# Cross-attention and routed experts on one core: four neighbouring rows per partition, VectorE gates each tile when it is ready, GpSimd makes the later expert numbers

## The reference

```python
x = x + xattn(layernorm(x), ctx_1024, W_q, W_kv, W_out, ln_gamma, ln_beta)   # 16 heads of 64, 77 context rows
x = x + ffn(layernorm(x), Wg, bg, W1, b1, W3, b3, W2, b2)                    # 8 experts, d_ff 512, top 2

# ffn
probs = softmax(x @ Wg + bg)
top_v, top_i = top_k(probs, 2);  top_v = top_v / (top_v.sum(-1) + 1e-6)
for e in range(8):
    h = silu(x @ W1[e] + b1[e]) * (x @ W3[e] + b3[e])
    out = out + combine[..., e:e+1] * (h @ W2[e] + b2[e])
```

## Time and profile before

| | |
|---|---|
| median of 3 runs | 160.51 us (160.01 to 161.1) |
| the profiled execution | 159.87 us, of which the span from its first to its last instruction is 157.9 us |
| TensorE busy, share of span | 143.5 us, 91% |
| VectorE busy | 103.3 us, 65% |
| ACT busy | 79.0 us, 50% |
| GpSimd busy | 80.9 us, 51% |
| chain that ended last | TensorE 72%, VectorE 10%, ACT 8%, DMA 3%, "issue" 3% |
| granted TensorE clock | 1.00 of full speed (2.4 GHz) over the span |

### The profile page before, as it was taken

One profiled execution on the slowest core, in us unless ns is written; L12 is line 12 of the kernel. 1 busy time (PEld: TensorE's weight loads), 2 busy tenths in 40 slices (PEclk: granted clock), 3 DMA queues, 4 the chain that ended last, 5 costly groups with the idle time before them and its releaser, 6 DMA issues.

```text
span 157.9 us, 4065 instructions
## 1 busy us (share of the span) xinstructions
PE 143.5 (91%) x1209; PEld 134.5 (85%) x1209; DVE 103.3 (65%) x319; ACT 79.0 (50%) x222; POOL 80.9 (51%) x98
## 2 busy tenths in 40 slices
PE   5986996989999999897989999999997999999990
PEld 5875885779998999896868899999996999999990
DVE  0548599989899977897759875365453363484350
ACT  3179357857464694830544243544754544535031
POOL 3550003948553686214781577777777777535000
PEclk9999999999999999999999999999999999999999
DMA  4999995130000003028953089878437996810454
GB/s 128 328 315 290 248 144 92 34 126 11 2 2 4 0 0 110 27 69 268 286 142 109 17 241 367 274 265 222 154 80 226 328 335 209 268 50 21 132 150 133
DMA packets 23821, 24.50 MB, mean 155 GB/s; under 512 B 2525, under 2 KB 16713, under 8 KB 23801
## 3 DMA queue, kind: packets, MB, share of 16 engines
q1 hardware_dynamic: 20608, 20.57, 44.4%
q0 software_dynamic: 1440, 2.82, 6.4%
q10 hardware_dynamic: 1753, 0.87, 2.0%
HBM read 19.91 MB, written 4.33 MB: 154 GB/s over the span
## 4 chain that ended last, share of the span: by engine, by line
PE 72%; DVE 10%; ACT 8%; DMA 3%; issue 3%; SPq 0%; ACTq 0%; DVEq 0%
PE psum L1378 26%; PE psum L1391 14%; PE psum L1439 9%; PE psum L1421 5%; DMA early<-in_L_xattn_W_kv_dram 3%; PE psum L1154 2%; PE psum L1405 2%; PE psum L1156 2%; PE psum L1155 2%; DVE prob L849 2%; DVE negmax L844 2%; ACT g_room L643 2%; PE psum L1365 2%; PE psum L1288 1%; DVE perm L929 1%
## 5 line engine op out<-in xcount | busy, mean ns | idle before, releaser
L1378 PE MATMUL psum<-probT,w 128*128 128x128 f32 x368 | 45.5, 276 | 2.8 <-issue 1.7
L1378 PEld LDWEIGHTS psum<-probT,w 128*128 128x128 f32 x368 | 43.0, 192 | 3.8 <-issue 2.7
L1096 DVE SCALAR_TENSOR_TENSOR probT<-psum,bias_col,prob 128x128 f32<-128x128 f32 x92 | 26.0, 345 | 28.3 <-ACT prob L743 27.6
L743 ACT ACTIVATE prob<-psum,bias_col 128x128 f32<-128x128 f32 x92 | 26.2, 368 | 35.1 <-PE psum L1378 35.1
L573 POOL DMA_INDIRECT g_room<-xf_scratch,idx x22 | 22.1, 1003 | 15.9 <-issue 6.0
L530 POOL TENSOR_TENSOR prob<-prob,rowsum 128x1232 f32<-128x1232 f32 x8 | 18.0, 2250 | 22.5 <-DVE rowsum L840 22.5
L1391 PE MATMUL psum<-w,probT 128*128 x184 | 25.0, 279 | 0.3 <-DVE probT L1096 0.2
L1391 PEld LDWEIGHTS psum<-w,probT 128*128 128x128 f32 x184 | 22.6, 191 | 0.9 <-issue 0.8
L582 POOL DMA_INDIRECT y_scratch<-xnT,out_row x16 | 16.4, 1023 | 9.8 <-DVE xnT L1105 6.4
L1439 PE MATMUL psum<-vo,probT 128*128 128x128 f32 (+1 forms) x160 | 19.3, 276 | 0.0
L1439 PEld LDWEIGHTS psum<-vo,probT 128*128 128x128 f32 (+1 forms) x160 | 18.5, 192 | 0.0
(11 more groups left out here) (186 smaller groups left out, 203.2 us busy)
## 6 DMA issues: line engine op xcount, KB each, us to landing
w<-in_L_ffn_W_dram SPq DMA_DIRECT2D x54, 256.0 KB, 5.2
early<-in_L_xattn_W_kv_dram SPq DMA_DIRECT2D x2, 512.0 KB, 6.2
y_scratch<-zero_rows SPq DMA_DIRECT2D x2, 512.0 KB, 8.4
x_sb<-in_x_dram SPq DMA_DIRECT2D x2, 256.0 KB, 5.0
early<-in_L_xattn_W_q_dram SPq DMA_DIRECT2D x1, 512.0 KB, 6.1
...
xf_scratch<-xf SPq DMA_DIRECT2D x2, 256.0 KB, 2.6
```

The source lines that it names most:

```text
L743: act.activation(silu[:, j % 2, c, :], psum[:, 2 * (j % 2), c * P:(c + 1) * P], ACT.Silu, bias=bias_col[:, 0, bass.ds(expert, 1), c]).then ...
L1096: dve.scalar_tensor_tensor(out=hT[:, j % 2, c, :], in0=psum[:, 2 * (j % 2) + 1, c * P:(c + 1) * P], scalar=bias_col[:, 1, bass.ds(expert[j ...
L1378: ins = pe.matmul(psum[:, 2 * (j % 2) + a, c * P:(c + 1) * P], w13[:, j % WR, a, c * P:(c + 1) * P], xt[:, j % XR, :], start=True, stop=True)
```

## The change

- **Layout.** Token p * 4 + t of a batch element stands on partition p of tile t: four neighbouring rows per partition. The loads of x, the stores to the scratch of xf, the reads of y_back and the stores of the output follow (`rows_of_half`), as do two constants of token numbers (`row_of`, `iota_n`).
- **Gate weights.** They are stored from `gate_w` as they stand, four numbers per partition, in four DMAs that wait for gate_ok. The transpose, the copy `gateT` and its semaphores go.
- **VectorE's order.** gated(0) follows top_two(2); the bases (`other_bases`) come out of other_tiles and follow gated(0); ranks(2) and blocks_of(2) stand before gated(1); other_tiles and one_hots(2) behind it; bias_down(0) and gated(2) stand before other_rows; the output rows come out of other_rows (`other_out_rows`) and stand behind gated(3).
- **Expert numbers of tiles 5 to 22.** `other_experts` moves from VectorE to GpSimd, as eight instructions, ahead of last_powers and gather(5).
- **Register loads.** VectorE reads the numbers of tiles 0 and 1 behind first_tiles, that of tile 2 behind other_bases; TensorE reads each tile's number right behind the up of the tile before.
- **TensorE's and ACT's order.** The slot rows of the other tiles come behind up(3) instead of up(2); from up(4) on, expert_xT(j + 1) follows up(j).

The diff, cut to what the text speaks of:

```diff
-        out_rows = out.rearrange("b (t p) d -> p (b t) d", p=P)
+        out_rows = out.rearrange("b (p t) d -> p b t d", p=P)
+        def rows_of_half(dram, k, half):
+            row = k * (N + P) + half * BANK
+            return dram[row:row + BANK, :].rearrange("(p t) d -> p t d", p=P)
         OWN_AT = [psum[:, RANK_BANK, :], psum[:, 6, :]]
-        GATE_AT = psum[0:K * T, RANK_BANK, 0:P]
         AFTER = 4
...
         def _(sp):
-            x_v = x.rearrange("b (t p) d -> p (b t) d", p=P)
-            sp.dma_start(x_sb[:, 0:TB, :], x_v[:, 0:TB, :]).then_inc(ld["x0"], 16)
+            x_v = x.rearrange("b (p t) d -> p b t d", p=P)
+            sp.dma_start(x_sb[:, 0:TB, :], x_v[:, 0, :, :]).then_inc(ld["x0"], 16)
             sp.dma_start(wkv_sb[:, 0:INNER], w_kv[:, 0:INNER]).then_inc(ld["wk"], 16)
             sp.dma_start(wq_sb, w_q[:, :]).then_inc(ld["wq"], 16)
-            sp.dma_start(x_sb[:, TB:T, :], x_v[:, TB:T, :]).then_inc(ld["x1"], 16)
+            sp.dma_start(x_sb[:, TB:T, :], x_v[:, 1, :, :]).then_inc(ld["x1"], 16)
             sp.dma_start(wkv_sb[:, INNER:2 * INNER], w_kv[:, INNER:2 * INNER]).then_inc(ld["wv"], 16)
...
                 for t in groups[2]:
-                    row = k * (N + P) + t * P
-                    sp.dma_start(xf_dram[row:row + P, :], zero_rows[:, :]).then_inc(zero_st, 16)
+                    sp.dma_start(rows_of_half(xf_dram, k, t // TB)[:, t % TB, :], zero_rows[:, :]).then_inc(zero_st, 16)
...
                 for k in range(K):
-                    row = k * (N + P) + g.start * P
-                    sp.dma_start(xf_dram[row:row + len(g) * P, :].rearrange("(t p) d -> p t d", p=P),
+                    sp.dma_start(rows_of_half(xf_dram, k, g.start // TB)[:, g.start % TB:g.start % TB + len(g), :],
                                  xf[:, g.start:g.stop, :]).then_inc(xf_st[n // 2], 16)
...
                 elif j == 2 * FULL + 4:
-                    sp.wait_ge(gateT_ok, 1)
+                    sp.wait_ge(gate_ok, 1)
                     for k in range(K):
-                        row = k * (N + P)
-                        sp.dma_start(gate_dram[row:row + N, :].rearrange("(t p) o -> t (p o)", p=P),
-                                     gateT[k * T:(k + 1) * T, :]).then_inc(gate_st, 16)
+                        for half in range(B):
+                            sp.dma_start(rows_of_half(gate_dram, k, half).rearrange("p t o -> p (t o)"),
+                                         gate_w[:, k, half * TB:(half + 1) * TB]).then_inc(gate_st, 16)
                 expert_weights(j)
...
             for k in range(K):
-                row = k * (N + P)
-                sp.dma_start(y_back[:, k, 0:TB, :],
-                             y_dram[row:row + BANK, :].rearrange("(t p) d -> p t d", p=P)).then_inc(back[0][k], 16)
+                sp.dma_start(y_back[:, k, 0:TB, :], rows_of_half(y_dram, k, 0)).then_inc(back[0][k], 16)
             sp.wait_ge(o_ok, 1)
-            sp.dma_start(out_rows[:, 0:TB, :], xn[:, 0:TB, :]).then_inc(stored, 16)
+            sp.dma_start(out_rows[:, 0, :, :], xn[:, 0:TB, :]).then_inc(stored, 16)
             sp.wait_ge(stored, 16 * B)
...
                           allow_small_or_imprecise_dtypes=True).then_inc(const_ok, 1)
-                pool.iota(row_of[:, :, :], pattern=[[P, T], [N + P, K]], base=-PAD_ROW, channel_multiplier=1,
+                pool.iota(row_of[:, :, :].rearrange("p (b t) k -> p b t k", b=B), pattern=[[BANK, B], [1, TB], [N + P, K]],
+                          base=-PAD_ROW, channel_multiplier=TB,
                           allow_small_or_imprecise_dtypes=True).then_inc(const_ok, 1)
...
                     pool.wait_ge(st_free, slot[("vo", len(vo_groups) - 1)] + 1)
-                    pool.iota(iota_n, pattern=[[1, N]], base=0, channel_multiplier=0,
+                    pool.iota(iota_n.rearrange("p (b t q) -> p b t q", b=B, t=TB), pattern=[[BANK, B], [1, TB], [TB, P]],
+                              base=0, channel_multiplier=0,
                               allow_small_or_imprecise_dtypes=True).then_inc(iota_n_ok, 1)
...
                                    shifted[:, FIRST:T, :].rearrange("p t e -> p (t e)"), ALU.pow).then_inc(expo_2_ok, 1)
+            def other_experts():
+                pool.wait_ge(base_ok, 1)
+                pool.tensor_tensor(end_e[:, :], base[0:1, :], padded[0:1, :], ALU.add).then_inc(p_eid, 1)
+                pool.wait_ge(p_eid, 1)
+                pool.tensor_tensor(end_e[:, :], end_e[:, :], taken_e[0:1, :], ALU.add).then_inc(p_eid, 1)
+                pool.wait_ge(p_eid, 2)
+                pool.tensor_tensor(ended[:, :, :], iota_j[0:1, FULL:NT].rearrange("p (j o) -> p j o", o=1).broadcast_to([1, NT - FULL, E]),
+                                   end_e[:, :].rearrange("p (o e) -> p o e", o=1).broadcast_to([1, NT - FULL, E]),
+                                   ALU.subtract).then_inc(p_eid, 1)
+                pool.wait_ge(p_eid, 3)
+                pool.tensor_scalar(ended[:, :, :], ended[:, :, :], 0.0, None, ALU.is_ge).then_inc(p_eid, 1)
+                pool.wait_ge(p_eid, 4)
+                for n, half in enumerate((4, 2)):
+                    pool.tensor_tensor(ended[:, :, 0:half], ended[:, :, 0:half], ended[:, :, half:2 * half], ALU.add).then_inc(p_eid, 1)
+                    pool.wait_ge(p_eid, 5 + n)
+                pool.tensor_tensor(eid_f[:, FULL:NT], ended[:, :, 0], ended[:, :, 1], ALU.add).then_inc(p_eid, 1)
+                pool.wait_ge(p_eid, 7)
+                pool.tensor_scalar(eid[:, FULL:NT], eid_f[:, FULL:NT], float(E - 1), None, ALU.min).then_inc(eid_ok, 1)
...
                 if j == FULL:
+                    other_experts()
                     last_powers()
...
-                pool.wait_ge(gate_st, 16 * (1 + K))
+                pool.wait_ge(gate_st, 16 * (1 + K * B))
                 for n in range(DIRECT):
...
             for j in range(2, NT):
-                if j + 1 < NT and j == 2:
+                if j == 2:
+                    expert_xT(3)
+                gate_silu(j)
+                if j == 2:
+                    expert_xT(4)
+                elif 4 <= j < NT - 1:
                     expert_xT(j + 1)
-                gate_silu(j)
-                if j + 2 < NT:
-                    expert_xT(j + 2)
                 if 0 <= j - (FULL + 5) < TB:
...
             for k in range(K):
-                row = k * (N + P) + BANK
-                act.dma_start(y_back[:, k, TB:T, :],
-                              y_dram[row:row + BANK, :].rearrange("(t p) d -> p t d", p=P)).then_inc(back[1][k], 16)
+                act.dma_start(y_back[:, k, TB:T, :], rows_of_half(y_dram, k, 1)).then_inc(back[1][k], 16)
             act.wait_ge(gate_ok, 1)
...
             act.wait_ge(o_ok_2, 1)
-            act.dma_start(out_rows[:, TB:T, :], xn[:, TB:T, :]).then_inc(stored, 16)
+            act.dma_start(out_rows[:, 1, :, :], xn[:, TB:T, :]).then_inc(stored, 16)
...
-            def other_tiles():
-                link(dve.tensor_copy(floor_2[:, PAIRS_1:T * K], floors[:, PAIRS_1:T * K]))
+            def other_bases():
+                dve.wait_ge(rk_mm, G)
                 link(dve.scalar_tensor_tensor(out=padded[:, :], in0=TOTALS[1], scalar=ROUND_128, in1=taken_r[:, :],
                                               op0=ALU.add, op1=ALU.subtract))
                 link(dve.tensor_tensor(low_pad[:, :, 0:E], lower[:, :, :], over_pairs(padded[:, :], E), ALU.mult))
-                link(dve.tensor_reduce(base[:, :], low_pad[:, :, :], AX.X, ALU.add))
+                dve.tensor_reduce(base[:, :], low_pad[:, :, :], AX.X, ALU.add).then_inc(base_ok, 1)
+                dve.wait_ge(base_ok, 1)
+            def other_tiles():
+                link(dve.tensor_copy(floor_2[:, PAIRS_1:T * K], floors[:, PAIRS_1:T * K]))
                 link(dve.tensor_tensor(based[:, :, :, :].rearrange("p t k e -> p (t k) e"), masks, over_pairs(base[:, :], T * K), ALU.mult))
...
-            def other_experts():
-                link(dve.tensor_tensor(end_e[:, :], base[0:1, :], padded[0:1, :], ALU.add))
-                link(dve.tensor_tensor(end_e[:, :], end_e[:, :], taken_e[0:1, :], ALU.add))
-                link(dve.tensor_tensor(ended[:, :, :], iota_j[0:1, FULL:NT].rearrange("p (j o) -> p j o", o=1).broadcast_to([1, NT - FULL, E]),
-                                       end_e[:, :].rearrange("p (o e) -> p o e", o=1).broadcast_to([1, NT - FULL, E]), ALU.is_ge))
-                link(dve.tensor_reduce(eid_f[:, FULL:NT], ended[:, :, :], AX.X, ALU.add))
-                dve.tensor_scalar(eid[:, FULL:NT], eid_f[:, FULL:NT], float(E - 1), None, ALU.min).then_inc(eid_ok, 1)
             def other_rows():
...
                 dve.tensor_scalar(idx[:, FULL:NT], OTHER_AT, row_base[:, 0:1], None, ALU.add).then_inc(idx_ok, 1)
+            def other_out_rows():
                 link(dve.scalar_tensor_tensor(out=unused[:, :], in0=OTHER_AT, scalar=0.0, in1=iota_pad[:, FULL:NT],
...
```

(65 more changed lines are left out.)

5 lines of the change are left out of this document (2 added, 3 removed).

## The result

The changed kernel takes 159.41 us (median of 20 executions, 156.62 to 161.23), the kernel before 160.38 us (20 executions, 159.91 to 162.9). By these medians it is faster by 0.6%. The ratio is 0.9844, with a 95% interval of 0.9814 to 0.9874; it leaves out executions over 1.5% above the fastest of their kernel, here 13 of the changed kernel's 20, so it is lower than 159.41 / 160.38. By the ratio 160.51 becomes 158.0, 1.5% less where 2.0% was forecast and inside the predicted range; the median of all executions lies 0.2 us above that range and above the 158.9 up to which the prediction called the kernel faster. Since the experiments trace most of the executions left out to the kernel itself, the 0.6% is what its user gets. The forecast of 157.3 is what the changed kernel takes in a few of its executions only.

What follows compares the result with a forecast made beforehand. TensorE sets the pace from up(5), leaving time before the tiles, tile losses and the tail to win. -1.5 - 1.0 - 0.2 - 0.5 = -3.2 us takes 159.87 to 156.7, given as 157.3 for the median; range 155.7 to 159.2.

Steps and rivals of the forecast that it cites:

- The gate stores: Near tile 14: SP's 5.8 us wait goes, weights again lead by three tiles (8.4 us), -1.5 us.
- rival 3: Near tile 14: the gate stores hold up the weights and it stalls as before; -1.8 us, 158.7 us, chance 0.08.
- The register loads: Ahead of the first tiles' idx on VectorE: two loads, 1.6 us against 0.55 cover, delay up(0) by 1.05 us.
- GpSimd: Ahead of gather(5): eight expert-number instructions take 3.0 us, hidden while idx comes later, cover 0.75 us.
- rival 1: Ahead of gather(5): GpSimd's instructions take over 3.8 us and the start wins nothing; -2.2 us, 158.3 us, chance 0.17.
- The rows of tile 5: Ahead of up(5): the new last event, gather 3.4 us, then 0.8 for transpose, copy and hand-over; up(5) at 93.75.
- the x load: At the chain's beginning: wider runs bring x sooner ahead of W_kv, -0.2 us, bounds 0 and 0.4 won.
- the start: Up to up(5): it begins at 93.75 instead of 94.75, a gain of 1.0 us net of the register loads.
- The steady tile: Whole expert tiles stay at 2.79 us, cost 0, with 0.03 us of cover a tile.
- rival 4: Every steady tile: the next tile's copy comes late, 1.8 us per 0.1; chance 0.10, 0.03 for slower by 1%.
- The tail: Last store and reads of y_back: wider runs shorten them, -0.5 us, bounds 0 and -1.0.
- stall: Near tile 14: up(13) to up(14) takes 4.10 us instead of 2.79; its removal is most of the -1.5 us.

Runs made afterwards that it cites:

- experiment 9: The changed kernel with down(3) ahead of tile 5's rows and weights held from tile 7 on until tile 5's gather landed: 156.26 us.
- Experiment 7: The changed kernel with the weights of tile 6 and all later ones held until the gather of tile 5 had landed: 157.16 us.
- experiment 10: The changed kernel with only the weights of tile 7 and all later ones held until the gather of tile 5 had landed: 156.00 us.
- experiment 2: The changed kernel with 14 unused transposes of the identity on TensorE behind up(4), in the wait for tile 5's rows: 158.97 us.
- experiment 12: The kernel of experiment 9 with VectorE's two first register loads moved behind top_two(2), just ahead of gated(0): 156.65 us.
- experiments 4: The kernel before with its gate stores issued ahead of the weights of tile 17 instead of those of tile 14: 159.25 us.
- experiment 6: The kernel before with the new orders and expert numbers on GpSimd alone, old layout and transposed gates kept: 161.36 us.
- experiment 5: The kernel before with four rows per partition and gate weights stored without a transpose, all orders as before: 157.82 us.

## Why the prediction was right, and where its sum was wrong

**The gate stores: right.** Forecast -1.5; from up(6) to the tail's first matmul (L1506, then L1540) it is 48.60 us (98.71 to 147.31) against 49.99 (97.54 to 147.53), -1.39. That matmul on the two chains, first before, then after:

```profile
147.53 0.89 PE psum L1506 x8
...
147.31 0.89 PE psum L1540 x8
```

The waits of SP's queue have none for gate weights now where the earlier trace rows had 5.8 us; its wait for a free place among the weights (L430), the rhythm of the ring, has 5.1 us as its longest:

```profile
SPq L430 <- PE psum L1409: 18.8, 13, 5.1
```

SP's timeline shows the four stores:

```profile
110.75 1.86 SPq L454 DMA_DIRECT2D gate_scratch<-gate_w  x4
```

They keep the queue 1.86 us, well inside the lead; rival 3 did not come. The Trainium skill's rule on transfers under 512 B ("DMA: Bandwidth & Descriptors", section "Specifications"), which stood beside that rival, is not refuted: whatever the small runs cost, no later row shows it.

**The register loads: right in time.** Forecast +1.05 by 1.6 us against 0.55 us of cover. On the chain of the changed kernel:

```profile
72.01 0.17 DVE key_in L992
72.20 0.56 DVEq L1075
72.79 0.20 DVEq L1075
73.11 0.31 DVEq L1075
73.46 0.19 DVEq L1075
73.75 0.22 DVE idx L1102
```

idx stands 1.58 us behind the end of key_in instead of 0.55: +1.03. The first load was 0.56 and not 0.73, the gaps made up for it. What was not seen is that the same 1.03 us become idle time of TensorE in one piece (0.33 to 1.36 us), behind which its clock can fall (experiment 9).

**GpSimd: right.** Forecast 3.0 us for the eight instructions, the pow done at 88.8 and a cover of 0.75:

```profile
82.02 0.20 POOL L565 TENSOR_TENSOR end_e<-base,padded 1x8 f32<-1x8 f32 x1 [0.80 <-DVE base L1027]
...
84.77 0.31 POOL L580 TENSOR_SCALAR eid<-eid_f 1x18 int32<-1x18 f32 x1
...
85.52 2.95 POOL L559 TENSOR_TENSOR expo<-base_e,shifted 128x16 f32<-128x16 f32 x1
89.11 1.10 POOL L594 DMA_INDIRECT g_room<-xf_scratch,idx  x1 [0.64 <-DVE idx L1048]
```

They took 3.06 us (82.02 to 85.08), the pow ended at 88.47, and GpSimd still waited 0.64 us for idx. No instruction was held as the one of 647 ns in the earlier trace rows seemed to be; rival 1 did not come. idx came at 88.59, forecast 89.05.

**The rows of tile 5: the step that failed.** The forecast had named them as the new last event, and was wrong on what follows. On the axis shifted by the x load (-0.2) up(5) was to start at 93.55 and up(6) at 96.34; they started at 94.73 and 98.71, 2.37 us late in all:

- the gather was issued 0.24 us earlier than forecast (89.11 for 89.35), less than the start alone moves from profile to profile (below, the x load);
- it landed in 4.06 us instead of 3.4: +0.66. In the kernel before the DMA engines were idle beside it (share 0.00 from 87 to 89 us) and it took 2.56 us; here their share was 0.67 to 1.04 (90 to 93 us). Experiment 7 shows that the company is the cause in this kernel: without it, 2.56 again. The company is the change's own doing, since GpSimd's earlier expert numbers let SP load the weights of tiles 5 to 8 at that moment. Its amount is not the whole of it: 3.31 us at shares of 0.84 and 0.80 (experiment 10), but 5.56 at 0.89 and 0.90 (experiment 2), and 4.35 in experiment 12 at 0.92, 0.53, 0.29 and 0.01. What sets the landing time beside transfers stays open. The Trainium skill, "DMA: Bandwidth & Descriptors", section "Latency and other measured facts", lets the memory's latency grow from 0.2 us on average to 2 us at high load; the added 0.75 to 3 us agree in direction only;
- from the landing to up(5) the forecast counted 0.8 us for transpose, copy and hand-over, and forgot that down(3) stands between them on TensorE: 1.12 us at full clock (experiment 7, 91.77 to 92.89 by the weight load), +0.3;
- the clock: down(3) and what is around it 0.4 us longer, tile 5 3.98 instead of 2.79, together +1.6.

The first three change the start by 0.7 us; the clock is the larger part, and no step of the prediction had it. Its rows all had a clock of 1.00, and it took a wait as costing its own length.

**The x load: not shown.** Forecast -0.2. key_in starts 0.14 us earlier in this pair of profiles, but it starts anywhere from 72.01 to 73.30 us in the profiles with the new layout and from 72.15 to 73.11 in those with the old one (the kernel before, experiments 4 and 6). On the changed kernel's chain the first products with W_kv follow 16 transposes of the identity (L1217), which take 2.06 us there and 3.35 in experiment 9, and no longer the load of W_kv.

**The steady tile: right**, 2.79; rival 4 did not come.

**The tail: right in kind, half in size.** Forecast -0.5, with 0 and -1.0 as bounds; from L1540 to the span's end it is 9.39 us against 10.37, -1.0. The last store, by the page's DMA issues (KB, us to landing):

```profile
out_dram<-xn ACTq DMA_DIRECT2D x1, 256.0 KB, 2.0
```

It lands in 2.0 us instead of 3.0; in experiment 5 too (2.0), in experiment 6 with the old layout not (3.0). Whether the longer runs do this or the other half's store, which is issued 0.74 us ahead of it now (153.49 and 154.23) and 0.17 before (154.27 and 154.44), no run parts. I had taken the middle of the bounds; the whole of the upper one came.

**The sum.** -3.2 + 2.4 (tile 5) + 0.1 (stall) - 0.5 (tail) = -1.2, which is the profiled execution: span 157.9 before, 156.7 after. The x load stands in it with the -0.2 forecast. In the four executions at clock 1.00 the median is 157.6, 0.3 above the forecast. That the result lies in the range at all is in part luck: the +2.4 us at tile 5 met 0.5 us more than forecast in the tail, and the 2.0 us left over are about the distance from the forecast to the range's upper end (157.3 to 159.2), which rival 3 had set, and rival 3 did not come.
